# GNN layer on one core: gamma in a wider centring matmul, and the loaded-column matmuls of the last three panels behind the row-tiled ones

## The chip, the cores and the metric

The kernel runs on one core of one Trainium2 chip. The metric is the device time of one execution in microseconds (us); the kernel before takes 407.3 us, the median of three runs (407.11 to 409.26).

## What is computed

All numbers are float32. N is 5120 nodes (2048 users, 3072 items), the embedding has 64 elements.

```python
h = jnp.maximum(_layernorm(x, axis=-1), 0.0)
# in the layer, with ego = res = h
u = par_u[0] * par_u[1] * (diag_u[:, None] * ego_u @ W_u) + ego_u
i = par_i[0] * par_i[1] * (diag_i[:, None] * ego_i @ W_i) + ego_i
e = jnp.concatenate([u, i], axis=0)
h = adj @ (adj.T @ e)
mu = jnp.mean(h, axis=-1, keepdims=True)
var = jnp.var(h, axis=-1, keepdims=True)
out = (h - mu) * jax.lax.rsqrt(var + LN_EPS) * ln_gamma + ln_beta + res
x = x + out
```

`adj` is 5120 x 5120, about 105 MB, and each element is used twice: in `t = adj.T @ e` and in `adj @ t`.

## The kernel before, in words

**Panels.** The columns of `adj` are cut into 20 panels of 256. For a panel, SP's queue loads five blocks of 1024 rows (`natural`, 1 MB each, L173), so that rows are on partitions, and for the last block the same numbers a second time with columns on partitions (`cols`, 1 MB, L177). Both have two buffers, picked by `a = g % 2`.

**A panel on TensorE.** `first` (L463) multiplies all five blocks with `e` and sums into `t_acc`: 40 matmuls of 256 columns, which write the two halves of the output partitions in turn. ScalarE copies the sum (`t_across`, L275), TensorE turns it (`t_turn`, L475), VectorE folds it into `t` (L379), and ScalarE spreads that over the four partition quadrants (`t_strips`, held in `centred`, L283). Then the panel is multiplied with `t` into `h_acc`: the first four row blocks by `second_strips` (L500), 64 matmuls in tiles of 32 rows, whose data VectorE has turned in 32 x 32 pieces (`strips`, L374); the fifth by `second_loaded` (L485), four matmuls of 512 columns straight from `cols`. In `step(g)` the order on TensorE is: `first(g)`, `second_loaded(g-1)`, `t_turn(g)`, `second_strips(g-1)`. Steps 2 to 17 are a loop with two panels in its body, 18 is written once more by `middle_steps` (L130 to L134), and panel 19, which is `LAST`, is written out at L555 to L565.

**The end.** `h_acc` now holds the transpose of h: banks 0 to 3 row blocks 0 to 3, cut by quadrants, and bank 4 (`LOADED`) block 4. ScalarE and VectorE copy the four banks into `h_across` (L319, L419), which lies over a dead part of `natural`, in two halves. `out_turn(m)` (L528) multiplies each piece of 128 columns of block m with `centre`. That turns the data back and subtracts the mean in one matmul, since `centre` is the identity minus 1/64 inside each half; its result lies in one bank, given by `out_bank(m)`. Block 4 comes by way of `across` (L323). Then, for each of the five blocks m: ScalarE squares (L313), VectorE sums the squares (L342), ScalarE takes the root (L249), VectorE multiplies the centred rows with gamma (L425), takes the reciprocal of the root (L347) and multiplies with it (L429). GpSimd adds the result to the residual `xs` (L231; for block 4 VectorE does, L432), and SP sends 256 KB to HBM (L198). TensorE's order in this stretch: `second_loaded(18)`, `out_turn(0)`, `out_turn(1)`, `second_loaded(19)`, `out_turn(2)` to `out_turn(4)`.

**What sets the order.** Each engine's program is written out by hand; engines meet only at semaphores. SP issues the loads in order: `load_natural(g, m)` waits for `first(g-2, m)` and for VectorE's turning of that block; `load_cols(g)` waits until `second_loaded` has been done g - 1 times. A late wait there holds back all loads behind it. The matmuls of float32 appear in the trace as two records each, with a weight load before each record.

Of the kernel before, what the change touches and what calls it, by code (L numbers as in the profile page):

```python
# [5 lines left out]
P = 128  # L6
N = 5120
D = 64
N_USERS = 2048
Q = 32  # L10
QUADRANTS = P // Q
ROWS = 1024
GROUPS = N // ROWS
# [23 lines left out]
def gnn_layer(nc, x, small, adj_rows, adj_cols, out):  # L37

    ctx = ExitStack()
    with ctx:  # L40
# [15 lines left out]
        ident = sb("ident", [P, P])  # L56
        centre = sb("centre", [P, P])
        smalls = sb("smalls", [P, SMALL])
# [18 lines left out]
        t_across = sb("t_across", [P, WIDE])  # L77
        t = sb("t", [P, 2, BLOCKS, D])
        t_strips = centred

        h_acc = ps("h_acc", [P, GROUPS, BANK])
# [5 lines left out]
        s_natural = [[sem(f"s_natural{a}{m}") for m in range(GROUPS)] for a in range(2)]  # L87
        s_cols = [sem(f"s_cols{a}") for a in range(2)]
        s_eps = sem("s_eps")
        s_idle = sem("s_idle")  # L90
# [32 lines left out]
        s_o_centred = sem("s_o_centred")  # L123
        s_o_gamma = sem("s_o_gamma")
        s_o_scaled = sem("s_o_scaled")
# [19 lines left out]

        def out_bank(m):

            return (t_acc[:, 0], t_acc[:, 1], h_acc[:, 0], h_acc[:, 1], h_acc[:, 2])[m]

# [17 lines left out]
        @block.sync  # L167
        def _(sp):
            sp.dma_start(xs[:, 0:GT, :], x[:, 0:GT, :]).then_inc(s_x[0], 16)
            sp.dma_start(smalls[:], small).then_inc(s_small, 16)  # L170

            def load_natural(g, m):
                sp.dma_start(natural[:, g % 2, m].rearrange("p t c -> p (t c)"),  # L173
                             adj_rows[g, m]).then_inc(s_natural[g % 2][m], 16)

            def load_cols(g):
                sp.dma_start(cols[:, g % 2].rearrange("p s b c -> p (s b c)"),  # L177
                             adj_cols[g]).then_inc(s_cols[g % 2], 16)

            for m in range(GROUPS):  # L180
                for g in range(2):
                    load_natural(g, m)
            for g in range(2):
                load_cols(g)
            for g in range(2, PANELS):
                for m in range(GROUPS):
                    sp.wait_ge(s_first, firsts_0(g - 2, m) if g < 4 else firsts(g - 2, m))
                    if m < TURNED:
                        sp.wait_ge(s_strips, TURNED * (g - 2) + m + 1)
                    load_natural(g, m)  # L190
                sp.wait_ge(s_loaded_done, g - 1)
                load_cols(g)
            for m in range(GROUPS):
                if m < LOADED:
                    sp.wait_ge(s_o_added, m + 1)
                else:
                    sp.wait_ge(s_o_done, 1)
                sp.dma_start(out[:, rows_of(m), :], xs[:, rows_of(m), :]).then_inc(s_out, 16)  # L198
            sp.wait_ge(s_out, 16 * GROUPS)

        @block.gpsimd
        def _(pool):
# [5 lines left out]
                                    pattern=[[-1, P]], channel_multiplier=1).then_inc(s_ident, 1)  # L208
            nc.gpsimd.memset(centre[:], 0.0).then_inc(s_zero, 1)
            for m in range(GROUPS):  # L210
# [12 lines left out]
            for d in range(2):  # L223
                half = slice(D * d, D * (d + 1))
                nc.gpsimd.memset(centre[half, half], -1.0 / D).then_inc(s_centre_part, 1)
            pool.wait_ge(s_centre_part, 2)
            nc.gpsimd.affine_select(out=centre[:], in_=centre[:], compare_op=ALU.not_equal, fill=1.0 - 1.0 / D,
                                    base=0, pattern=[[-1, P]], channel_multiplier=1).then_inc(s_centre, 1)
            for m in range(LOADED):
                pool.wait_ge(s_o_scaled, m + 1)  # L230
                nc.gpsimd.tensor_tensor(residual(m), scaled[:, m % 2].rearrange("p (k s) d -> p k s d", s=2),  # L231
                                        residual(m), ALU.add).then_inc(s_o_added, 1)

        @block.scalar
        def _(act):
# [41 lines left out]
            def spread_t(g, a):  # L277

                act.wait_ge(s_t, g + 1)
                for c in range(QUADRANTS):  # L280
                    for q in range(QUADRANTS):
                        into = t_strips[Q * q:Q * (q + 1), a].rearrange("p (b c) d -> p b c d", c=QUADRANTS)
                        last = nc.scalar.copy(into[:, :, c], t[Q * c:Q * (c + 1), a])  # L283
                last.then_inc(s_t_strips, 1)
# [21 lines left out]
            middle_steps(act, step)  # L306
            step(LAST, LAST % 2, LAST // 2)

            def square_out(m):
                n = GROUPS + m  # L310
                act.wait_ge(s_o_centred, m + 1)
                act.wait_ge(s_var, n - 1)
                nc.scalar.activation(squares[:, n % 2], out_bank(m).rearrange("p (k d) -> p k d", d=D),  # L313
                                     ACT.Square).then_inc(s_squares, 1)
                std(n)

            act.wait_ge(s_strips_last, 1)
            for half in range(2):
                nc.scalar.copy(*strips_across(half, 0)).then_inc(s_o_low, 1)  # L319
            square_out(0)  # L320
            square_out(1)
            act.wait_ge(s_loaded_done, PANELS)
            nc.scalar.copy(across[:, 0], h_acc[:, LOADED]).then_inc(s_o_loaded, 1)  # L323
            for m in range(2, GROUPS):
                square_out(m)

        @block.vector
        def _(dve):
# [47 lines left out]

            def keep_t(g, a):
                dve.wait_ge(s_t_turned, g + 1)
                nc.vector.tensor_reduce(t[:, a], t_turned[:, 0:2 * WIDE // 2].rearrange("p (b s d) -> p b d s",  # L379
                                                                                       b=BLOCKS, s=2),  # L380
                                        AX.X, ALU.add).then_inc(s_t, 1)

            def step(g, a, half):
                for m in range(TURNED):
                    turn_strips(g, a, half, m)
                keep_t(g, a)

# [23 lines left out]
            for g in range(2):  # L411
                keep_t(g, g)
            for m in range(TURNED):
# [4 lines left out]
            for half in range(2):  # L418
                nc.vector.tensor_copy(*strips_across(half, 2)).then_inc(s_o_high, 1)  # L419
            gamma_rows = gamma_s.unsqueeze(1).to_broadcast([P, GT, D])  # L420
            for m in range(GROUPS):
                sum_squares(GROUPS + m)
                if m >= 2:
                    dve.wait_ge(s_o_added, m - 1)
                nc.vector.tensor_tensor(scaled[:, m % 2], out_bank(m).rearrange("p (k d) -> p k d", d=D),  # L425
                                        gamma_rows, ALU.mult).then_inc(s_o_gamma, 1)
                r = inverse_deviation(GROUPS + m)
                dve.wait_ge(s_o_gamma, m + 1)
                nc.vector.tensor_tensor(scaled[:, m % 2], scaled[:, m % 2], r, ALU.mult).then_inc(s_o_scaled, 1)  # L429
            dve.wait_ge(s_o_scaled, GROUPS)  # L430
# [5 lines left out]
        def _(pe):  # L436
# [42 lines left out]
            def second_loaded(g, a, half):  # L479

                pe.wait_ge(s_cols[a], 16 * (half + 1))
                pe.wait_ge(s_t, g + 1)
                for b in range(BLOCKS):
                    for s in range(2):
                        last = nc.tensor.matmul(h_acc[D * s:D * (s + 1), LOADED], t[:, a, b, :], cols[:, a, s, b],  # L485
                                                start=(isinstance(g, int) and g == 0 and b == 0),
# [20 lines left out]
            def step(g, a, half):  # L507
                for m in range(GROUPS):
                    first(g, a, half, m)
                second_loaded(g - 1, 1 - a, half - 1 + a)  # L510
                t_turn(g)
                second_strips(g - 1, 1 - a).then_inc(s_strips_done, 1)

            def out_turn(m):

                if m == 0:
                    pe.wait_ge(s_centre, 1)
                    pe.wait_ge(s_t_across, PANELS)
                if m == LOADED:
                    pe.wait_ge(s_o_loaded, 1)  # L520
                else:
                    half = 0 if m < 2 else 1
                    pe.wait_ge(s_o_low, half + 1)
                    pe.wait_ge(s_o_high, half + 1)
                for k in range(HALF):
                    part = across[:, 0, P * k:P * (k + 1)] if m == LOADED else h_across[:, m, k].rearrange(
                        "p q i -> p (q i)")
                    last = nc.tensor.matmul(out_bank(m)[:, P * k:P * (k + 1)], part, centre[:], start=True, stop=True)  # L528
                last.then_inc(s_o_centred, 1)
# [25 lines left out]
            for m in range(GROUPS):  # L555
                first(LAST, LAST % 2, LAST // 2, m)
            t_turn(LAST)
            second_strips(LAST - 1, 0).then_inc(s_strips_done, 1)
            second_strips(LAST, 1).then_inc(s_strips_last, 1)
            second_loaded(LAST - 1, 0, LAST // 2)  # L560
            out_turn(0)
            out_turn(1)
            second_loaded(LAST, 1, LAST // 2)
            for m in range(2, GROUPS):
                out_turn(m)  # L565

# [35 lines left out]
```

## Time and profile before

| | |
|---|---|
| median of 3 runs | 407.3 us |
| profiled execution | 407.53 us |
| its span, first to last instruction | 405.7 us |
| mean granted TensorE clock | 0.986 |
| TensorE matmul busy | 382.7 us (94%) |
| VectorE busy | 219.6 us (54%) |
| ScalarE busy | 125.6 us (31%) |
| GpSimd busy | 19.9 us (5%) |
| HBM read | 127.36 MB |

The busy share is an average over the span; the stretch that the change touches begins at about 356 us, where it has to be read anew. PE is TensorE's matmuls, PEld its weight loads, DVE VectorE, ACT ScalarE, POOL GpSimd, SP the engine that issues the loads. The ends of matmul records are modelled.

### The profile page before, as it was taken

The page shows a single profiled execution, that of the slowest core. Times are in us where ns is not written, and L with a number is a line of the kernel's source. Part 1 is how long each engine was busy: PE and PEld are TensorE (multiplying, and loading weights), DVE is VectorE, ACT ScalarE, POOL GpSimd, SP SyncE. Part 2 cuts the span into 40 slices and gives each one's busy share as a digit, 9 for nine tenths or more (in the row PEclk, how much of TensorE's full clock was granted, in tenths as well). Part 3 has the DMA queues.
Part 4 walks back from the last instruction along what each step waited for, and adds up shares of the span by engine and source line. Part 5 has one row for each costly group of instructions (what it writes and reads, how often), then busy time and mean ns, then how long its engine had stood idle before and what let it go on. Part 6 is the DMA issues. An engine that isn't in the chain of part 4 may idle for free.

```text
span 405.7 us, 10226 instructions
## 1 busy us (share of the span) xinstructions
PE 382.7 (94%) x4524; PEld 197.0 (49%) x4524; DVE 219.6 (54%) x160; ACT 125.6 (31%) x410; POOL 19.9 (5%) x26
## 2 busy tenths in 40 slices
PE   5679799999999999999999999999999999999991
PEld 2446345455454645445464545546354554535451
DVE  5677658365471827446281735538183653719047
ACT  4434550413405041331504042250504224050422
POOL 1211700000000000000000000000000000000013
PEclk9989989999999999999999999999999999999997
DMA  8999895979897987979797897979789797940003
GB/s 315 422 422 419 331 417 211 357 299 395 329 428 292 387 332 304 414 295 427 291 420 300 327 392 300 428 284 428 296 348 376 291 427 291 426 155 2 3 1 129
DMA packets 18879, 128.89 MB, mean 318 GB/s; under 512 B 2096, under 2 KB 2224, under 8 KB 3504
## 3 DMA queue, kind: packets, MB, share of 16 engines
q1 hardware_dynamic: 18288, 127.63, 77.7%
q10 hardware_dynamic: 576, 1.05, 0.7%
q8 instruction: 11, 0.18, 0.2%
q14 instruction: 4, 0.03, 0.0%
HBM read 127.36 MB, written 1.31 MB: 317 GB/s over the span
## 4 chain that ended last, share of the span: by engine, by line
PE 87%; DVE 6%; ACT 4%; issue 2%; DMA 1%; DVEq 0%; ACTq 0%
PE t_acc L463 41%; PE h_acc L500 35%; PE h_acc L485 8%; ACT h_in L260 2%; PE t_turned L475 2%; ACT centred L283 1%; DVE var L342 1%; DMA xs<-x 1%; DVE scaled L429 1%; DVE e L366 1%; DVE scaled L425 1%; DVE strips L374 1%; DVE total L331 0%; PE h_acc L443 0%; DVE centred L337 0%
## 5 line engine op out<-in xcount | busy, mean ns | idle before, releaser
L374 DVE STREAM_TRANSPOSE strips<-natural 128x2048 f32<-128x2048 f32 x80 | 178.1, 2281 | 118.8 <-PE h_acc L500 118.8
L463 PE MATMUL t_acc<-natural,e 128*64 128x256 f32 x1600 | 180.6, 383 | 6.0 <-DVE e L366 6.0
L463 PEld LDWEIGHTS t_acc<-natural,e 128*64 128x64 f32 x1600 | 112.4, 137 | 77.8 <-issue 16.0
L500 PE MATMUL h_acc<-strips,centred 32*64 32x512 f32 x2560 | 143.9, 596 | 2.7 <-ACT centred L283 2.7
L283 ACT COPY centred<-t 32x128 f32<-32x128 f32 x320 | 94.5, 295 | 41.3 <-DVE t L379 37.7
L500 PEld LDWEIGHTS h_acc<-strips,centred 32*64 32x64 f32 x2560 | 55.9, 133 | 77.8 <-issue 77.8
L275 ACT COPY t_across<-t_acc 128x256 f32<-128x256 f32 x20 | 7.4, 372 | 195.8 <-PE t_acc L463 194.0
L485 PE MATMUL h_acc<-cols,t 128*64 128x512 f32 x160 | 37.9, 594 | 0.0
L379 DVE TENSOR_REDUCE t<-t_turned 128x128 f32<-128x256 f32 x20 | 8.5, 425 | 35.0 <-PE t_turned L475 35.0
L231 POOL TENSOR_TENSOR xs<-scaled,xs 128x512 f32<-128x512 f32 x4 | 5.1, 1272 | 347.2 <-DVE scaled L429 347.2
L485 PEld LDWEIGHTS h_acc<-cols,t 128*64 128x64 f32 x160 | 11.2, 137 | 15.0 <-issue 12.4
L475 PEld LDWEIGHTS t_turned<-ident,t_across 128*128 128x128 f32 x40 | 4.0, 140 | 15.9 <-issue 14.2
L260 ACT ACTIVATE h_in<-centred,rstd 128x64 f32<-128x64 f32 x40 | 10.2, 337 | 0.0
L337 DVE SCALAR_TENSOR_TENSOR centred<-total,xs 128x512 f32<-128x512 f32 x5 | 6.7, 1348 | 6.1 <-ACT h_in L260 6.1
L475 PE MATMUL t_turned<-ident,t_across 128*128 128x128 f32 x40 | 8.7, 300 | 1.1 <-DVE t L379 0.6
L419 DVE COPY natural<-h_acc 128x512 f32<-128x512 f32 x2 | 1.3, 686 | 13.6 <-PE h_acc L500 13.6
L213 POOL TENSOR_TENSOR xs<-xs,h_in 128x512 f32<-128x512 f32 x5 | 6.3, 1267 | 33.6 <-ACT h_in L260 33.6
L342 DVE TENSOR_REDUCE var<-squares 128x8 f32<-128x512 f32 x10 | 6.7, 674 | 2.2 <-ACT squares L313 2.2
L536 PE MATMUL h_acc<-across 32*64 32x512 f32 x64 | 5.2, 803 | 1.8 <-POOL across L204 1.8
L269 ACT COPY across<-h_acc 128x512 f32<-128x512 f32 x5 | 2.9, 581 | 12.3 <-PE h_acc L443 12.3
L453 PE MATMUL h_acc<-smalls,across 128*128 128x128 f32 x40 | 5.8, 287 | 0.9 <-ACT across L269 0.9
L218 POOL TENSOR_TENSOR xs<-xs,smalls 128x512 f32<-128x512 f32 x5 | 6.2, 1267 | 0.0
(39 smaller groups left out, 58.7 us busy)
## 6 DMA issues: line engine op xcount, KB each, us to landing
natural<-adj_rows SPq DMA_DIRECT2D x100, 1024.0 KB, 10.9
cols<-adj_cols SPq DMA_DIRECT2D x20, 1024.0 KB, 4.8
out<-xs SPq DMA_DIRECT2D x5, 256.0 KB, 2.0
xs<-x ACTq DMA_DIRECT2D x4, 256.0 KB, 5.9
xs<-x SPq DMA_DIRECT2D x1, 256.0 KB, 3.5
smalls<-small SPq DMA_DIRECT2D x1, 214.0 KB, 4.2
```

The source lines that it names most:

```text
L213: nc.gpsimd.tensor_tensor(xs[:, rows_of(m), :], xs[:, rows_of(m), :], h_in[:, m % 2], ALU.add).then_inc(s_res_part, 1)
L260: last = nc.scalar.activation(h_in[:, m % 2, k], centred[:, m % 2, k], ACT.Relu, scale=rstd[:, m % 2, k:k + 1])
L275: nc.scalar.copy(t_across[:], t_acc[:, a, 0:WIDE]).then_inc(s_t_across, 1)
L283: last = nc.scalar.copy(into[:, :, c], t[Q * c:Q * (c + 1), a])
L337: nc.vector.scalar_tensor_tensor(centred[:, m % 2], by_tile(total[:, m % 2]), -1.0 / D, xs[:, rows_of(m), :], ALU.mult, ALU.add).then_inc( ...
L342: nc.vector.tensor_reduce(var[:, n % 2], squares[:, n % 2], AX.X, ALU.add).then_inc(s_var, 1)
L374: nc.vector.transpose(strips[:, a, :, m].rearrange("p c t i -> p t c i"), natural[:, a, m].rearrange("p t (c j) -> p t c j", j=Q)).then_in ...
L379: nc.vector.tensor_reduce(t[:, a], t_turned[:, 0:2 * WIDE // 2].rearrange("p (b s d) -> p b d s", b=BLOCKS, s=2), AX.X, ALU.add).then_inc( ...
L463: last = nc.tensor.matmul(t_acc[D * s:D * (s + 1), a, 0:WIDE], e[:, GT * m + HALF * s + k, :], natural[:, a, m, HALF * s + k], start=(m == ...
L475: last = nc.tensor.transpose(t_turned[:, P * b:P * (b + 1)], t_across[:, P * b:P * (b + 1)], ident[:])
L485: last = nc.tensor.matmul(h_acc[D * s:D * (s + 1), LOADED], t[:, a, b, :], cols[:, a, s, b], start=(isinstance(g, int) and g == 0 and b == 0),
L500: last = nc.tensor.matmul(h_acc[D * s:D * (s + 1), q], t_strips[part, a, c, :], rows, start=(isinstance(g, int) and g == 0 and c == 0), st ...
```

## The change

- **Gamma.** `centre` becomes twice as wide. Its first 128 columns are as before, its second 128 columns are the same matrix with each column multiplied by its gamma (made once on GpSimd, behind the building of `centre`). `out_turn` multiplies with all 256 columns, so it gives the centred rows and, beside them, the centred rows times gamma. The result of a block now takes a pair of banks (`out_banks`). ScalarE squares the first part. VectorE multiplies the second part with the reciprocal; its own multiplication by gamma (L425) is gone.
- **Waits for banks.** `out_turn(1)` waits for both halves of the copies, `out_turn(3)` for the scaling of block 0, and `out_turn(4)` for that of block 1.
- **Order.** `step(18)` no longer calls `second_loaded(17)`. At the end TensorE runs `second_loaded(17)`, `out_turn(0)`, `out_turn(1)`, `second_loaded(18)`, `out_turn(2)`, `out_turn(3)`, `second_loaded(19)`, `out_turn(4)`. `t` gets a third buffer, used by panel 19.
- **The last load of columns.** The column-major data of panel 19 goes into `cols_last`, which lies over `natural[:, 0, 1]`, and is loaded when `first(18, 1)` and the turning of that block are done, not when `second_loaded` has been done 18 times.

The core of the diff (semaphore declarations, slices of `centre` and the passing of the buffer number left out):

```diff
-        def out_bank(m):
-
-            return (t_acc[:, 0], t_acc[:, 1], h_acc[:, 0], h_acc[:, 1], h_acc[:, 2])[m]
+        def out_banks(m):
+
+            pair = (t_acc[:, 0:2], h_acc[:, 0:2], h_acc[:, 2:4], t_acc[:, 0:2], h_acc[:, 0:2])[m]
+            return pair.rearrange("p n (k f c) -> p (n k) f c", k=2, f=2)
...
-                sp.wait_ge(s_loaded_done, g - 1)
-                load_cols(g)
+                if g < LAST:
+                    sp.wait_ge(s_loaded_done, g - 1)
+                    load_cols(g)
+            sp.wait_ge(s_first, firsts(LAST - 1, 1))
+            sp.wait_ge(s_strips, TURNED * (LAST - 1) + 2)
+            sp.dma_start(cols_last.rearrange("p s b c -> p (s b c)"), adj_cols[LAST]).then_inc(s_cols_last, 16)
...
+            pool.wait_ge(s_centre, 1)
+            nc.gpsimd.tensor_tensor(centre[:, 1].rearrange("p (s d) -> p s d", s=2),
+                                    centre[:, 0].rearrange("p (s d) -> p s d", s=2),
+                                    gamma_s.unsqueeze(1).to_broadcast([P, 2, D]), ALU.mult).then_inc(s_centre, 1)
...
-                nc.scalar.activation(squares[:, n % 2], out_bank(m).rearrange("p (k d) -> p k d", d=D),
+                nc.scalar.activation(squares[:, n % 2].rearrange("p (k s) d -> p k (s d)", s=2), out_banks(m)[:, :, 0],
...
-            square_out(0)
-            square_out(1)
-            act.wait_ge(s_loaded_done, PANELS)
-            nc.scalar.copy(across[:, 0], h_acc[:, LOADED]).then_inc(s_o_loaded, 1)
-            for m in range(2, GROUPS):
+            for m in range(GROUPS):
+                if m == LOADED:
+                    act.wait_ge(s_loaded_done, PANELS)
+                    nc.scalar.copy(across[:, 0], h_acc[:, LOADED]).then_inc(s_o_loaded, 1)
                 square_out(m)
...
-                nc.vector.tensor_tensor(scaled[:, m % 2], out_bank(m).rearrange("p (k d) -> p k d", d=D),
-                                        gamma_rows, ALU.mult).then_inc(s_o_gamma, 1)
-                r = inverse_deviation(GROUPS + m)
-                dve.wait_ge(s_o_gamma, m + 1)
-                nc.vector.tensor_tensor(scaled[:, m % 2], scaled[:, m % 2], r, ALU.mult).then_inc(s_o_scaled, 1)
+                nc.vector.tensor_tensor(scaled[:, m % 2].rearrange("p (k s) d -> p k s d", s=2),
+                                        out_banks(m)[:, :, 1].rearrange("p k (s d) -> p k s d", s=2), r,
+                                        ALU.mult).then_inc(s_o_scaled, 1)
...
-                second_loaded(g - 1, 1 - a, half - 1 + a)
+                if not isinstance(g, int):
+                    second_loaded(g - 1, 1 - a, half - 1 + a)
...
+                if m == 1:
+                    pe.wait_ge(s_o_low, 2)
+                    pe.wait_ge(s_o_high, 2)
+                if m >= 3:
+                    pe.wait_ge(s_o_scaled, m - 2)
...
-                    last = nc.tensor.matmul(out_bank(m)[:, P * k:P * (k + 1)], part, centre[:], start=True, stop=True)
+                    last = nc.tensor.matmul(out_banks(m)[:, k], part, centre[:], start=True, stop=True)
...
-            second_loaded(LAST - 1, 0, LAST // 2)
+            second_loaded(LAST - 2, 1, LAST // 2 - 1)
             out_turn(0)
             out_turn(1)
+            second_loaded(LAST - 1, 0, LAST // 2)
+            out_turn(2)
+            out_turn(3)
             second_loaded(LAST, 1, LAST // 2)
-            for m in range(2, GROUPS):
-                out_turn(m)
+            out_turn(LOADED)
```

## Rows read from the trace of the kernel before

**Rows 1.** The profile's page, part 2: tenths in 40 slices of the span.

```profile
PE   5679799999999999999999999999999999999991
DVE  5677658365471827446281735538183653719047
PEclk9989989999999999999999999999999999999997
```

**Rows 2.** Chain of waits, 355 to 375 us: start us, us, what.

```profile
355.92 1.72 PE h_acc L485 x8
357.64 0.37 PE t_turned L475 x2
358.01 7.05 PE h_acc L500 x128
365.06 8.81 PE t_acc L463 x80
373.87 0.02 issue
373.89 0.38 ACT t_across L275
374.27 0.04 issue
374.32 0.44 PE t_turned L475 x2
```

**Rows 3.** Chain of waits, the end.

```profile
392.30 0.69 DVE var L342
392.98 0.60 DVE scaled L425
393.58 0.12 DVE rstd L347
393.72 0.69 DVE scaled L429
394.42 0.60 DVE var L342
...
401.84 0.70 DVE scaled L429
402.54 0.02 issue
402.57 0.69 DVE xs L432
```

**Rows 4.** Instructions in order of time, the end: start us, us, engine, line.

```profile
388.60 1.94 PE L485 MATMUL h_acc<-cols,t 128*64 128x512 f32 x8
390.47 2.05 PE L528 MATMUL t_acc<-centre,natural 128*128 128x128 f32 x16
391.67 0.60 ACT L313 ACTIVATE squares<-t_acc 128x512 f32<-128x512 f32 x1 [1.81 <-PE t_acc L528]
392.45 1.94 PE L485 MATMUL h_acc<-cols,t 128*64 128x512 f32 x8
392.90 0.68 DVE L425 TENSOR_TENSOR scaled<-t_acc,smalls 128x512 f32<-128x512 f32 x1
393.02 0.30 ACT L249 ACTIVATE var<-var,eps 128x8 f32<-128x8 f32 x1 [0.75 <-DVE var L342]
393.50 0.19 DVE L347 RECIPROCAL rstd<-var 128x8 f32<-128x8 f32 x1
395.26 0.56 ACT L323 COPY across<-h_acc 128x512 f32<-128x512 f32 x1
396.21 1.06 PE L528 MATMUL h_acc<-centre,across 128*128 128x128 f32 x8
```

**Rows 5.** Busy time by stretch: window, us, PE, PEld, DVE, ACT, POOL, clock, DMA share, GB/s.

```profile
388.60:397.40 8.80, 8.67 (x64) 5.58 (x56) 6.33 (x12) 4.05 (x10) 2.15 (x2) 1.00 0.08 31
397.40:405.70 8.30, 0.00 (x0) 0.00 (x0) 5.72 (x12) 1.54 (x4) 2.94 (x3) 0.71 0.33 126
```

**Rows 6.** Instructions in order of time, 364.5 to 374.5 us.

```profile
364.99 8.85 PE L463 MATMUL t_acc<-natural,e 128*64 128x256 f32 x80
365.24 8.89 DVE L374 STREAM_TRANSPOSE strips<-natural 128x2048 f32<-128x2048 f32 x4 [6.77 <-PE h_acc L500]
```

**Rows 7.** Instructions in order of time: SP and DVE, 340 to 358 us.

```profile
340.19 2.65 SPq L173 DMA_DIRECT2D natural<-adj_rows  x5
347.32 6.70 DVE L374 STREAM_TRANSPOSE strips<-natural 128x2048 f32<-128x2048 f32 x3 [6.77 <-PE h_acc L500]
357.68 0.33 SPq L177 DMA_DIRECT2D cols<-adj_cols  x1
```

**Rows 8.** DMAs of L173 (340 to 343 us) and L177 (357 to 358 us).

```profile
DMA to landing us min/median/max: 6.9/10.9/14.6
DMA to landing us min/median/max: 4.7/4.7/4.7
```

**Rows 9.** Instructions of one line (L528, L485, L463): ns min/median/max, first and last start.

```profile
L528 PEld LDWEIGHTS t_acc<-centre,natural x16: 186/192/192, 390.5 to 392.1; 128*128 128x128 f32 x16
L528 PE MATMUL t_acc<-centre,natural x16: 275/275/377, 390.5 to 392.2; 128*128 128x128 f32 x16
L485 PE MATMUL h_acc<-cols,t x16: 592/592/643, 388.6 to 393.8; 128*64 128x512 f32 x16
L463 PE MATMUL t_acc<-natural,e x80: 379/379/430, 365.0 to 373.5; 128*64 128x256 f32 x80
```

**Rows 10.** GpSimd, start of the span: the work behind which the widening stands.

```profile
49.25 0.29 POOL L227 TENSOR_SCALAR_AFFINE_SELECT centre<-centre 128x128 f32<-128x128 f32 x1
```

More of the change, by code:

```diff
@@ L56, in gnn_layer @@
         ident = sb("ident", [P, P])
-        centre = sb("centre", [P, P])
+        centre = sb("centre", [P, 2, P])
         smalls = sb("smalls", [P, SMALL])
@@ L77, in gnn_layer @@
         t_across = sb("t_across", [P, WIDE])
-        t = sb("t", [P, 2, BLOCKS, D])
+        t = sb("t", [P, 3, BLOCKS, D])
         t_strips = centred
+        cols_last = natural[:, 0, 1].rearrange("p t c -> p (t c)").rearrange("p (s b c) -> p s b c", s=2, b=BLOCKS)
         h_acc = ps("h_acc", [P, GROUPS, BANK])
@@ L88, in gnn_layer @@
         s_cols = [sem(f"s_cols{a}") for a in range(2)]
+        s_cols_last = sem("s_cols_last")
         s_eps = sem("s_eps")
@@ L123, in gnn_layer @@
         s_o_centred = sem("s_o_centred")
-        s_o_gamma = sem("s_o_gamma")
         s_o_scaled = sem("s_o_scaled")
@@ L208, in _ @@
                                     pattern=[[-1, P]], channel_multiplier=1).then_inc(s_ident, 1)
-            nc.gpsimd.memset(centre[:], 0.0).then_inc(s_zero, 1)
+            nc.gpsimd.memset(centre[:, 0], 0.0).then_inc(s_zero, 1)
             for m in range(GROUPS):
@@ L224, in _ @@
                 half = slice(D * d, D * (d + 1))
-                nc.gpsimd.memset(centre[half, half], -1.0 / D).then_inc(s_centre_part, 1)
+                nc.gpsimd.memset(centre[half, 0, half], -1.0 / D).then_inc(s_centre_part, 1)
             pool.wait_ge(s_centre_part, 2)
-            nc.gpsimd.affine_select(out=centre[:], in_=centre[:], compare_op=ALU.not_equal, fill=1.0 - 1.0 / D,
+            nc.gpsimd.affine_select(out=centre[:, 0], in_=centre[:, 0], compare_op=ALU.not_equal, fill=1.0 - 1.0 / D,
                                     base=0, pattern=[[-1, P]], channel_multiplier=1).then_inc(s_centre, 1)
+            pool.wait_ge(s_centre, 1)
+            nc.gpsimd.tensor_tensor(centre[:, 1].rearrange("p (s d) -> p s d", s=2),
+                                    centre[:, 0].rearrange("p (s d) -> p s d", s=2),
+                                    gamma_s.unsqueeze(1).to_broadcast([P, 2, D]), ALU.mult).then_inc(s_centre, 1)
             for m in range(LOADED):
@@ L279, in spread_t @@
                 act.wait_ge(s_t, g + 1)
+                into_t = t[:, 2 if isinstance(g, int) and g == LAST else a]
                 for c in range(QUADRANTS):
@@ L282, in spread_t @@
                         into = t_strips[Q * q:Q * (q + 1), a].rearrange("p (b c) d -> p b c d", c=QUADRANTS)
-                        last = nc.scalar.copy(into[:, :, c], t[Q * c:Q * (c + 1), a])
+                        last = nc.scalar.copy(into[:, :, c], into_t[Q * c:Q * (c + 1)])
                 last.then_inc(s_t_strips, 1)
@@ L306, in _ @@
             middle_steps(act, step)
-            step(LAST, LAST % 2, LAST // 2)
+            step(LAST, 1, LAST // 2)
             def square_out(m):
@@ L375, in turn_strips, with keep_t @@
                                     natural[:, a, m].rearrange("p t (c j) -> p t c j", j=Q)).then_inc(s_strips, 1)
-            def keep_t(g, a):
+            def keep_t(g, a, into):
                 dve.wait_ge(s_t_turned, g + 1)
-                nc.vector.tensor_reduce(t[:, a], t_turned[:, 0:2 * WIDE // 2].rearrange("p (b s d) -> p b d s",
+                nc.vector.tensor_reduce(t[:, into], t_turned[:, 0:2 * WIDE // 2].rearrange("p (b s d) -> p b d s",
                                                                                        b=BLOCKS, s=2),
@@ L385, in step @@
                     turn_strips(g, a, half, m)
-                keep_t(g, a)
+                keep_t(g, a, 2 if isinstance(g, int) and g == LAST else a)
             row_sums(0)
@@ L411, in _ @@
             for g in range(2):
-                keep_t(g, g)
+                keep_t(g, g, g)
             for m in range(TURNED):
@@ L419, in _ @@
                 nc.vector.tensor_copy(*strips_across(half, 2)).then_inc(s_o_high, 1)
-            gamma_rows = gamma_s.unsqueeze(1).to_broadcast([P, GT, D])
             for m in range(GROUPS):
                 sum_squares(GROUPS + m)
+                r = inverse_deviation(GROUPS + m).rearrange("p (k s) d -> p k s d", s=2)
                 if m >= 2:
                     dve.wait_ge(s_o_added, m - 1)
-                nc.vector.tensor_tensor(scaled[:, m % 2], out_bank(m).rearrange("p (k d) -> p k d", d=D),
-                                        gamma_rows, ALU.mult).then_inc(s_o_gamma, 1)
-                r = inverse_deviation(GROUPS + m)
-                dve.wait_ge(s_o_gamma, m + 1)
-                nc.vector.tensor_tensor(scaled[:, m % 2], scaled[:, m % 2], r, ALU.mult).then_inc(s_o_scaled, 1)
+                nc.vector.tensor_tensor(scaled[:, m % 2].rearrange("p (k s) d -> p k s d", s=2),
+                                        out_banks(m)[:, :, 1].rearrange("p k (s d) -> p k s d", s=2), r,
+                                        ALU.mult).then_inc(s_o_scaled, 1)
             dve.wait_ge(s_o_scaled, GROUPS)
@@ L479, in second_loaded @@
             def second_loaded(g, a, half):
-                pe.wait_ge(s_cols[a], 16 * (half + 1))
+                if isinstance(g, int) and g == LAST:
+                    pe.wait_ge(s_cols_last, 16)
+                    lhs, rhs = t[:, 2], cols_last
+                else:
+                    pe.wait_ge(s_cols[a], 16 * (half + 1))
+                    lhs, rhs = t[:, a], cols[:, a]
                 pe.wait_ge(s_t, g + 1)
@@ L484, in second_loaded @@
                     for s in range(2):
-                        last = nc.tensor.matmul(h_acc[D * s:D * (s + 1), LOADED], t[:, a, b, :], cols[:, a, s, b],
+                        last = nc.tensor.matmul(h_acc[D * s:D * (s + 1), LOADED], lhs[:, b, :], rhs[:, s, b],
                                                 start=(isinstance(g, int) and g == 0 and b == 0),
@@ L516, in out_turn @@
                 if m == 0:
-                    pe.wait_ge(s_centre, 1)
+                    pe.wait_ge(s_centre, 2)
                     pe.wait_ge(s_t_across, PANELS)
@@ L555, in _ @@
             for m in range(GROUPS):
-                first(LAST, LAST % 2, LAST // 2, m)
+                first(LAST, 1, LAST // 2, m)
             t_turn(LAST)
```

## The prediction

> **What bounds the kernel now.** I read the slices of the page first: TensorE is at 9 tenths or more from the seventh slice to the last but one, at full clock, and in the last slice it is at 1 while VectorE is at 7 [rows 1]. So there are two stretches with different limits, and the change touches both. The chain of waits says where they meet. Up to 388.6 us it is TensorE matmul after matmul [rows 2]; from 392.3 us to the end it is VectorE, which does four operations for each of the five blocks of the output: the sum of squares, gamma, the reciprocal, the scaling [rows 3]. A block begins every 2.1 us there (392.30, 394.42; over all four steps it is 2.03). In between stand the matmuls of the end in order of time [rows 4]. TensorE's last record ends at 396.21 + 1.06 = 397.27, and VectorE's last at 402.57 + 0.69 = 403.26. The table by stretch shows the same: TensorE is busy for 8.67 of the 8.80 us up to 397.4 and not at all afterwards [rows 5]. So VectorE bounds the end, but TensorE is full until shortly before it. The question is what happens when VectorE's work is cut and TensorE's is raised there.
>
> **Part 1: `second_loaded(17)` leaves step 18.** It takes 1.72 us of the chain, and then `t_turn` follows with 0.37: 2.09 from 355.92 to 358.01 [rows 2]. But it also hid ScalarE's copy of `t_across`, for which `t_turn` waits. Panel 19 already runs without cover: 0.02 + 0.38 + 0.04 of waiting and then 0.44, together 0.88 [rows 2]. The step is shortened by 2.09 - 0.88 = **1.21 us**. Bounds: 0, if another wait takes its place, to 1.72, if the copy cost nothing. I take 1.21, since panel 19 is the same sequence without cover.
>
> What could be late 1.21 us earlier? The four turnings of panel 19 start when the strips of panel 17 are done (365.24, 0.2 behind them) and take 8.89 us beside the 8.81 us of `first(19)` [rows 2, 6]. Both ends move together. The `natural` blocks of panel 19 were issued from 340.19 on and landed after 14.6 us at most; even counted from the last issue (342.84) that is 357.4, and `first(19)` would need them at 365.06 - 1.21 = 363.85 [rows 2, 7, 8].
>
> **Part 2: the last load of columns.** It was issued at 357.68 and landed 4.7 us later [rows 7, 8]. Now it waits for the second turning of panel 18; three began at 347.32 and took 6.70, so the second ends near 351.8. That is earlier than before, while the `natural` blocks are still landing, and may push the last of them back by its own 4.7 us at most, to 362.1, still before 363.85. It is itself wanted at about 398 (part 4) and not at 392.45. Nothing behind it on SP's queue is wanted before the first output. Cost 0 to 0; had it no cover, up to 4.7.
>
> **Part 3: the centring matmuls.** This is the term that decides. A block has four matmuls, eight records. Sixteen records of 128 columns start from 390.47 to 390.47 + 2.05 - 0.275 = 392.25, which is 0.10 once and then 0.112 a record [rows 4, 9]. A 256-column record with the full array is not in the trace. The nearest rows are L463: 256 columns, 128 rows, but half of the output partitions, two records side by side. 80 records start within 8.85 - 0.38 = 8.47 us, so 40 pairs have 0.215 us each [rows 6, 9]. The `cols` matmuls have 512 columns, and eight records (four pairs) take from 388.60 to 390.47 with the change of form, 0.43 a pair [rows 4]. So a pass costs 0.84 ns a column in both, and 0.112 us is what 128 columns cost at that price, plus 0.005. The durations say the same of the full array: 275 ns for 128 columns, 379 for 256 and 592 for 512, which is 104 and 213 more for 128 and 256 more columns [rows 9]. The ends are modelled, but the engine that waits confirms the 275: the eighth centring record ends at 390.47 + 0.10 + 7 x 0.112 + 0.275 = 391.63, and ScalarE starts at 391.67 [rows 4]. Bounds for a wide record: 0.112 (the wider stream costs nothing, because something else sets the 0.112) and 0.215. I take 0.215. A block then takes 1.72 us of TensorE and not 0.89, five of them 4.1 us more.
>
> The page "TensorE: Matmul & The Clock Gate" of the Trainium skill speaks for the other bound. Its section on LDWEIGHTS gives the columns divided by 1.2 ns, 107 ns for 128 columns, as much as the spacing of the centring records; its section on the back-to-back gap gives N/2.4 + 2.5 ns, 109 ns for N = 256. By the two together the weight load would set the pace and the second 128 columns would be free. The trace disagrees with the gap as far as it goes: 256 columns stand at 215 ns and 512 at 430. No row of a full-array record decides it, so it stays a rival.
>
> **Part 4: the end put together**, on the old time axis, without part 1. `second_loaded(17)` stands where that of 18 stood, 388.60 to 390.47, and covers the copies as before. A pair of blocks in the wide form takes 0.10 + 16 x 0.215 + 0.10 for the change of form = 3.64, where the narrow pair took 392.45 - 390.47 = 1.98. So `second_loaded(18)` starts at 394.11, `out_turn(2)` at 395.98 (+1.87), `second_loaded(19)` at 399.62, and its last record ends at 401.56 (+1.94) [rows 4]. ScalarE's copy for block 4 (0.56 [rows 4]), with 0.04 on each side, lets `out_turn(4)` start at 402.20. Its last record starts 0.10 + 7 x 0.215 = 1.61 later and takes 0.38: 404.19. Then +0.04 the square, and +0.63 from there to the sum (391.67 to 392.30): 404.86. From the sum on nothing hides anything: 0.72 to the root (392.30 to 393.02), 0.30 root and 0.04, 0.19 reciprocal and 0.03 (before, only 0.12 of the reciprocal was outside cover), 0.72 scaling with its hand-over (401.84 to 402.57), 0.69 the residual: 2.69 [rows 3, 4]. End 407.55, where it was 403.26: **+4.29 us**.
>
> Is VectorE the bound instead? Without gamma its period is 0.72 + 0.30 + 0.04 + 0.22 + 0.69 less the 0.1 overlap of the next sum, 1.88: the root on ScalarE, which gamma had hidden, comes into the open, and of gamma's 0.68 only 0.15 a block is saved. Five blocks from 392.30 + 0.83 (the first block is also late by 0.83) bring the fifth sum to 400.65. TensorE's 404.86 is later by 4.2. The waits for `s_o_scaled` 1 and 2 are met near 395.1 and 397, before `out_turn(3)` (397.7) and `out_turn(4)`: 0.
>
> Two small things: ScalarE's copy stands behind the root of block 3. That block's matmuls end near 399.7, square and sum take it to 401.2, the root to 401.6, a tie with 401.56; up to 0.1. And GpSimd's widening of `centre` comes behind L227 at 49.25 [rows 10], 340 us before it is used, and is hidden: 0.
>
> **Sum.** -1.21 + 4.29 = +3.08 us, to which the 0.1 of the tie gives 3.1. Behind VectorE's last instruction the same 256 KB output follows. 407.53 + 3.1 = 410.6; the profiled execution lies 0.2 above the median of the runs, so 410.5 as a median.
>
> **Rivals.**
> 1. *The wide stream is free* (0.112 a record). `second_loaded(18)` starts at 392.45, that of 19 at 396.30 and ends at 398.24; `out_turn(4)` starts at 398.88 and ends at 400.04; sum at 400.71, end at 403.40. That is +0.14 - 1.21 = -1.07, and 406.3 as a median: not slower. For it: 0.112 is at one form only, and the weight loads between the records keep the same spacing (390.5 to 392.1 for sixteen), so it could be they that set it [rows 9]. Against it: the durations and L463. It is decided by the price of a record, since 39 of them stand on the path to the end of `out_turn(4)` behind the first: with 1.07 us in hand the break-even is 0.112 + 1.07/39 = 0.14, and 0.5% (2.0 us) slower is crossed at 0.19.
> 2. *The middle gives nothing*: another wait, such as the turning on VectorE (8.89 beside 8.81 [rows 2, 6]), takes the place of `second_loaded(17)`. Then 410.5 + 1.2 = 411.7. Against it: VectorE starts its turnings at the end of the strips, which moves too.
> 3. *The clock falls in the end.* It was 1.00 until 397.4, with TensorE 8.67 of 8.80 us busy, and fell only after TensorE had stopped [rows 5]. TensorE now works on to 404, with a hole of 0.6 before `out_turn(4)`. At the lower level (1.2 GHz) that block's 1.7 us would double: 412.2. The whole end shows no reason for it.
> 4. *The DMA*: the early column load displaces `natural` by more than its own time: up to 411.5; the two slacks above speak against it.
>
> **How the numbers follow.** Forecast 0.80, own range 409.7 to 411.4. Rival 1 0.12, with the prices in between, 406.3 to 409.5. Rivals 2 and 4 together 0.05, rival 3 0.03. The range 409.1 to 411.9 leaves out rival 1 nearly whole and the far end of rival 3. About 0.5% (2.0 us) is what a measurement of this kernel can tell from no change: slower from 409.3 on. Slower 0.77 (the forecast but for the part that noise in the runs could take under 409.3, and rivals 2 to 4), same 0.19 (rival 1 and that part), faster 0.04 (rival 1 with a middle that gives more).
>
> **What would show it.** Right: L528's records, now 128x256, at 379 ns and 0.215 apart; no L485 between L463 and L475 of panel 18, with 0.4 us of waiting for L275 there; the strips of panel 19 ending 1.2 us earlier, at 387.4; TensorE busy almost to 403; VectorE idle before each sum; the chain of the end going through L485 and L528 of block 4. Wrong: wide records 0.112 apart; L485 of panel 19 waiting for `cols_last`; VectorE's period still the chain of the end; the end of the last strips where it was.

## Result and profile after

The changed kernel takes 410.48 us (median of 20 executions, 408.61 to 412.46), the kernel before 407.25 us (20, 405.21 to 409.26). The ratio is 1.0076, 95% interval 1.0055 to 1.0098: slower by 3.1 us (2.2 to 4.0). That is over the 0.5% that the prediction named as what can be told from no change. The numbers in the table are read from one profiled execution of each kernel.

| profiled execution | before | after |
|---|---|---|
| span | 405.7 us | 409.4 us |
| first(18)'s end to the end of the last strips | 32.75 | 31.55 |
| from there to VectorE's last instruction | 14.59 | 18.95 |
| TensorE's last record, behind the last strips | 8.6 | 15.6 |
| VectorE busy, share of the span | 54% | 53% |

The second and third row are read from the chain of waits. First its part around panel 18 in the kernel after (start us, us, what), to be compared with [rows 2]:

```profile
356.48 0.02 issue
356.50 0.38 ACT t_across L285
356.88 0.04 issue
356.92 0.44 PE t_turned L483 x2
357.36 7.05 PE h_acc L513 x128
364.41 8.81 PE t_acc L471 x80
```

The 1.72 us of `second_loaded` are gone, and the wait for ScalarE's copy stands in their place, as panel 19 had it before. From 356.48 to 357.36 are 0.88 us, where [rows 2] had 2.09. Nothing behind it became later.

Then the end of the same chain, to be compared with [rows 3]:

```profile
374.11 13.92 PE h_acc L513 x256
388.03 1.87 PE h_acc L498 x8
389.89 1.93 PE t_acc L547 x8
391.82 1.73 PE h_acc L547 x8
393.55 1.87 PE h_acc L498 x8
395.41 1.92 PE h_acc L547 x8
397.34 1.73 PE t_acc L547 x8
399.06 1.89 PE h_acc L498 x8
...
400.98 0.59 ACT across L334
401.57 0.04 issue
401.62 2.01 PE h_acc L547 x8
...
403.65 0.61 ACT squares L324
...
404.28 0.70 DVE var L352
...
405.00 0.31 ACT var L259
...
405.33 0.21 DVE rstd L357
...
405.57 0.70 DVE scaled L435
...
406.29 0.69 DVE xs L440
```

VectorE's five blocks are no longer in the chain; only the last one is. In front of it stands TensorE with three blocks of columns (1.87 to 1.89) and five centrings: 1.73 behind another centring, 1.92 or 1.93 behind a block of columns, 2.01 for the last, which follows a wait of 0.67 for ScalarE's copy. All this, the wait included, goes from 388.03 to 403.62, which is 15.6 us. The pieces follow each other without a gap but for that one wait, so the new waits for banks cost TensorE nothing that the chain shows. The centring records by line (ns min/median/max, first and last start), to be compared with [rows 9]:

```profile
L547 PEld LDWEIGHTS t_acc<-centre,natural x16: 186/190/190, 389.8 to 398.5; 128*128 128x128 f32 x16
L547 PE MATMUL t_acc<-centre,natural x16: 379/379/483, 389.8 to 398.7; 128*128 128x256 f32 x16
```

They take 379 ns, as long as the 256-column records of half the output partitions in [rows 9], and not 275. The ends of these records are modelled, but their starts say the same: eight records take 1.73 us in the chain, 0.216 each.

What VectorE waits for now, in order of time (start us, us, engine, line; the bracket is the idle time before it):

```profile
392.49 0.69 DVE L352 TENSOR_REDUCE var<-squares 128x8 f32<-128x512 f32 x1 [3.06 <-ACT squares L324]
...
393.54 0.20 DVE L357 RECIPROCAL rstd<-var 128x8 f32<-128x8 f32 x1 [0.37 <-ACT var L259]
...
398.00 0.69 DVE L352 TENSOR_REDUCE var<-squares 128x8 f32<-128x512 f32 x1 [1.65 <-ACT squares L324]
...
404.28 0.69 DVE L352 TENSOR_REDUCE var<-squares 128x8 f32<-128x512 f32 x1 [2.40 <-ACT squares L324]
```

It waits 0.37 us for the root of its own block, which gamma used to hide, and 1.65 and 2.40 us ahead of the sums of blocks 2 and 4, whose squares wait for TensorE. The last load of columns was issued at 352.42, landed 7.5 us later, is first read at 398.99, and is not in the chain:

```profile
352.42 0.33 SPq L198 DMA_DIRECT2D natural<-adj_cols  x1
```

**The rest of the span.** The span grew by 3.7 us, the two stretches by -1.20 + 4.36 = 3.16. The rest is from the start: `first(18)` ends at 356.48 and not at 355.92, 0.56 later. The change does not touch that part but for one small instruction on GpSimd. By stretch (window, us, PE, PEld, DVE, ACT, POOL, clock, DMA share, GB/s), the first 60 us of the kernel before:

```profile
0.00:60.00 60.00, 45.93 (x424) 24.38 (x424) 39.88 (x47) 28.28 (x91) 14.85 (x22) 0.94 0.96 387
```

and of the kernel after:

```profile
0.00:60.00 60.00, 47.68 (x416) 25.54 (x424) 39.87 (x47) 28.29 (x91) 15.31 (x23) 0.91 0.92 370
```

VectorE and ScalarE do the same in both, while TensorE's granted clock is 0.94 in one and 0.91 in the other, and it is busy for 1.75 us more. I take the 0.56 for chance of the execution: in the profiles of the kernels below, six of which have that GpSimd instruction and none another change in the start, the start came out both shorter and longer than in the kernel before (last section). So the effect of the change is 3.16 us, and the ratio (3.1) and the difference of the medians (3.2) agree with it.

### The profile page after: what moved, and what is told of

It is laid out like the page before. It is cut to its first block, busy times and chain, and to the rows that moved or that the text cites. A ratio compares the mean times of both kernels' runs of the same rounds, so it can differ in the third digit from the quotient of the medians.

```text
span 409.4 us, 10223 instructions
## 1 busy us (share of the span) xinstructions
PE 389.7 (95%) x4524; PEld 200.9 (49%) x4524; DVE 217.2 (53%) x155; ACT 126.2 (31%) x410; POOL 20.4 (5%) x27
## 4 chain that ended last, share of the span: by engine, by line
PE 89%; ACT 4%; DVE 2%; issue 2%; DMA 1%; DVEq 0%; ACTq 0%
PE t_acc L471 42%; PE h_acc L513 34%; PE h_acc L498 8%; ACT h_in L270 2%; PE t_turned L483 2%; PE h_acc L547 1%; ACT centred L294 1%; PE t_acc L547 1%; DMA xs<-x 1%; DVE e L376 1%; PE h_acc L451 1%; DVE centred L347 0%; DVE var L352 0%; DVE total L341 0%; ACT t_across L285 0%
## 5 line engine op out<-in xcount | busy, mean ns | idle before, releaser
L513 PE MATMUL h_acc<-strips,centred 32*64 32x512 f32 x2560 | 142.2, 590 | 2.7 <-ACT centred L294 2.7
L498 PE MATMUL h_acc<-cols,t 128*64 128x512 f32 x152 | 36.0, 594 | 0.0
L555 PE MATMUL h_acc<-across 32*64 32x512 f32 x64 | 6.5, 976 | 1.8 <-POOL across L210 1.8
L461 PEld LDWEIGHTS h_acc<-smalls,across 128*128 128x128 f32 x40 | 5.4, 211 | 2.6 <-ACT across L279 1.5
```

Of the source, the lines that this page charges most:

```text
L461: last = nc.tensor.matmul(h_acc[:, m, P * b:P * (b + 1)], across[:, m % 2, P * b:P * (b + 1)], wdiag[:, int(m >= USER_GROUPS)], start=True ...
L498: last = nc.tensor.matmul(h_acc[D * s:D * (s + 1), LOADED], lhs[:, b, :], rhs[:, s, b], start=(isinstance(g, int) and g == 0 and b == 0), ...
L513: last = nc.tensor.matmul(h_acc[D * s:D * (s + 1), q], t_strips[part, a, c, :], rows, start=(isinstance(g, int) and g == 0 and c == 0), st ...
```

## Experiments

For each, the two stretches of the table above are given ("middle" and "end", for the kernel before 32.75 and 14.59), since they are free of the start. They come from one profile a kernel. Where two kernels should agree in a stretch they do so to 0.01 us (31.55 or 31.56 in five kernels, 32.75 in three), so I read differences of 0.1 us from them. The measured ratios to the kernel before stand beside them; their intervals are 0.4% to 0.5% wide, which is 1.6 to 2.2 us. The diffs are cuts, against the changed kernel, but for two whose text says against what.

### Only the wide centring

The order of matmuls, loads and ScalarE's copy as before; the gamma part is as changed. Of the edit only TensorE's order is shown.

```diff
-            second_loaded(LAST - 2, 1, LAST // 2 - 1)
+            second_loaded(LAST - 1, 0, LAST // 2)
             out_turn(0)
             out_turn(1)
-            second_loaded(LAST - 1, 0, LAST // 2)
-            out_turn(2)
-            out_turn(3)
             second_loaded(LAST, 1, LAST // 2)
-            out_turn(LOADED)
+            for m in range(2, GROUPS):
+                out_turn(m)
```

> Only the wide centring, in the old order of matmuls and loads. Theory A (the 256-column records cost 0.216 us where the 128-column ones cost 0.112, and TensorE, not VectorE, then ends last): from the end of the last strips, out_turn(2) to out_turn(4) run from 395.98 on the old axis without a break, the last ends at 401.43, and VectorE ends at 404.8 where it was 403.26: +1.5 us against the kernel before, with the step of panel 18 unchanged. Rival B (the order is what costs, the width little): within 0.5 us of before. Neither gives more than half of the +3.2 of the whole change.

Middle 32.75, end 16.46: +1.87 us. Ratio 1.0019 (0.9994 to 1.0043); the stretches say 1.0046, just above the interval, whose executions also hold the changing start. This is the one kernel where the two disagree by more than the interval, and that stays open. TensorE ran as forecast, but the end was 0.33 longer than expected (VectorE's end at 404.8 where it was 403.26, +1.54), and against the expectation it was VectorE that bounded the last two blocks:

```profile
398.95 0.70 DVE var L348
...
399.67 0.31 ACT var L255
...
400.00 0.21 DVE rstd L353
...
400.24 0.69 DVE scaled L431
400.93 0.60 DVE var L348
...
401.55 0.31 ACT var L255
...
401.89 0.21 DVE rstd L353
...
402.12 0.69 DVE scaled L431
402.82 0.60 DVE var L348
```

From block 2 on VectorE is again the bound: its sums start 1.89 apart (400.93, 402.82), TensorE's blocks come every 1.73. That is the period that the prediction gave to VectorE without gamma, 1.88, and it beats 2.03 by only 0.15. So the width alone makes TensorE deliver later, and VectorE catches up nearly nothing of it.

### Only the order

Centring 128 columns wide and gamma on VectorE as before, without the new waits for banks; all else as changed. Of the edit the matmul is shown.

```diff
-                    last = nc.tensor.matmul(out_banks(m)[:, k], part, centre[:], start=True, stop=True)
+                    last = nc.tensor.matmul(out_bank(m)[:, P * k:P * (k + 1)], part, centre[:, 0], start=True, stop=True)
```

> Only the order (second_loaded(17) to the end, the late load of columns, ScalarE's copy for block 4 behind block 3), with the centring 128 columns wide and gamma on VectorE. Theory A: -1.21 us in the step of panel 18. In the end ScalarE copies block 4 only behind the root of block 3 (399.40 on the old axis), out_turn(4) runs 400.04 to 401.20, and the fifth sum starts at 401.87 where it was 400.42: +1.45. Together +0.2 us against before. Rival B (the order is what costs): +2 us or more.

Middle 31.55, end 15.92: -1.20 + 1.33 = +0.13 us. Ratio 0.9997 (0.9975 to 1.0019). The middle is as in the changed kernel. What was gained there is given back at the end, and the chain names the place:

```profile
397.17 0.61 DVE var L352
...
397.80 0.03 ACT var L259
397.82 0.18 issue
398.01 0.57 ACT across L334
398.58 0.04 issue
398.63 1.17 PE h_acc L544 x8
```

ScalarE's copy for block 4 waits on its engine behind the root of block 3, which waits for VectorE's sum of block 3; TensorE stands still for the copy.

### The order, and ScalarE's copy earlier

As the kernel with only the order, but ScalarE copies block 4 between the square and the root of block 3.

```diff
-                if m == LOADED:
+                if m == LOADED - 1:
+                    act.wait_ge(s_o_centred, m + 1)
+                    act.wait_ge(s_var, GROUPS + m - 1)
+                    nc.scalar.activation(squares[:, (GROUPS + m) % 2], ...)
                     act.wait_ge(s_loaded_done, PANELS)
                     nc.scalar.copy(across[:, 0], h_acc[:, LOADED]).then_inc(s_o_loaded, 1)
-                square_out(m)
+                    std(GROUPS + m)
+                else:
+                    square_out(m)
```

> As the order alone, but ScalarE copies block 4 between the square and the root of block 3. Theory A: the copy then starts when second_loaded(19) is done (398.28 on the old axis), the fifth sum at 400.71: +0.29 and -1.21, together -0.9 us against before. If instead TensorE's fourth block of columns itself were the limit of the end, the copy's place would change nothing and it would be as the order alone (+0.2).

Middle 31.55, end 14.92: -0.87 us. Ratio 0.9972 (0.9947 to 0.9996). One place in ScalarE's order was worth 1.00 us, and the extra block of columns at the end costs 0.33 and not 1.87, since TensorE had the rest in hand.

### The changed kernel with the narrow centring, gamma left out

This one leaves gamma out of the result, and the waits for banks too; it shows what the changed kernel would be if the second 128 columns were free.

```diff
-                                        out_banks(m)[:, :, 1].rearrange("p k (s d) -> p k s d", s=2), r,
+                                        out_bank(m).rearrange("p (k s d) -> p k s d", s=2, d=D), r,
```

> The changed kernel with the centring 128 columns wide again and gamma left out of the result altogether: what the wide stream costs, all else as changed. Theory A: VectorE's period is 1.9 us (the root is in the open), ScalarE's copy comes behind the root of block 3 at 399.0 on the old axis, and the end is at 404.1: +0.9 and -1.21, together -0.35 us against before and 3.5 below the changed kernel. Rival B (width costs little): at most 1 us below the changed kernel.

Middle 31.56, end 15.43: -0.35 us, as expected. Ratio 0.9993 (0.9973 to 1.0012). The width alone, all else as changed, thus costs 18.95 - 15.43 = 3.52 us, against 3.5 expected. Its chain again has the copy behind the root of block 3:

```profile
399.04 0.03 ACT var L258
399.06 0.18 issue
399.25 0.57 ACT across L333
399.82 0.04 issue
399.86 1.17 PE h_acc L541 x8
```

### The kernel before with the cover split

The diff is against the kernel before. Besides what it shows, ScalarE copies block 4 between the square and the root of block 3, as in the kernel with the early copy.

```diff
-            second_loaded(LAST - 1, 0, LAST // 2)
+            second_loaded(LAST - 1, 0, LAST // 2, range(0, 1))
             out_turn(0)
             out_turn(1)
+            second_loaded(LAST - 1, 0, LAST // 2, range(1, 2))
+            out_turn(2)
+            out_turn(3)
             second_loaded(LAST, 1, LAST // 2)
-            for m in range(2, GROUPS):
-                out_turn(m)
+            out_turn(LOADED)
```

> The kernel before, with narrow centring and gamma on VectorE; in the end only half of second_loaded(18) stands ahead of the first two centrings and half behind, blocks 2 and 3 are centred ahead of second_loaded(19), and ScalarE copies block 4 ahead of the root of block 3. Theory A (VectorE bounds the end of the kernel before and TensorE has over 2 us in hand there): VectorE's chain starts 0.86 us earlier, since the copies need 0.9 of the 1.87 us that the matmuls covered; the end is 0.86 shorter, 13.7 us from the last strips to VectorE's last and not 14.6. If TensorE bounded the end, splitting its work would give nothing.

Middle 32.75, end 13.72: -0.87 us. Ratio 0.9983 (0.9959 to 1.0007). In its chain the cover is 1.01 and not 1.87, and VectorE starts its first sum 2.76 behind the last strips instead of 3.63:

```profile
388.54 1.01 PE h_acc L490 x4
389.55 1.10 PE t_acc L534 x8
...
390.67 0.60 ACT squares L313
...
391.30 0.69 DVE var L347
```

VectorE is in the chain without a break from there on, so the other two moves in this edit (blocks 2 and 3 ahead of `second_loaded(19)`, the copy later) cost and gain nothing. Here VectorE is the bound, and what starts it earlier is worth its full size.

### The order with the cover split

`second_loaded(17)` is cut in the same way in the kernel with the order and the early copy, against which the diff is.

```diff
-            second_loaded(LAST - 2, 1, LAST // 2 - 1)
+            second_loaded(LAST - 2, 1, LAST // 2 - 1, range(0, 1))
             out_turn(0)
             out_turn(1)
+            second_loaded(LAST - 2, 1, LAST // 2 - 1, range(1, 2))
             second_loaded(LAST - 1, 0, LAST // 2)
```

> The order alone with the early copy, and second_loaded(17) split around the first two centrings. Theory A: there TensorE bounds the end (it works for 11.4 us behind the last strips), so starting VectorE 0.86 earlier gives nothing: the end stays at 14.9 us, within 0.15, and the whole at -0.9 against before. If VectorE still bounded the end, it would be 14.1.

Middle 31.55, end 14.92, the same as without the split. Ratio 0.9986 (0.9963 to 1.0009). The same edit that gave 0.87 gives 0.00 where TensorE is the bound.

### Half of the block moved

Half of `second_loaded(17)` stays in step 18, the other half is the cover at the end; narrow centring, gamma on VectorE, early copy.

```diff
-                if not isinstance(g, int):
-                    second_loaded(g - 1, 1 - a, half - 1 + a)
+                second_loaded(g - 1, 1 - a, half - 1 + a, range(1 if isinstance(g, int) else BLOCKS))
...
-            second_loaded(LAST - 2, 1, LAST // 2 - 1)
+            second_loaded(LAST - 2, 1, LAST // 2 - 1, range(1, 2))
```

> The order of the changed kernel with narrow centring and gamma on VectorE, but only half of second_loaded(17) goes to the end, as the cover of the copies; the other half stays in step 18 and covers ScalarE's copy of t_across. Theory A: -0.86 us in the middle; in the end VectorE starts 0.86 earlier, but the fifth block is late by 0.27 from TensorE: -0.59. Together -1.45 us against before and 1 us or less against the order alone with the early copy. If the middle gives nothing with the cover kept, -0.6.

Middle 31.89, end 14.06: -0.86 - 0.53 = -1.39 us. Ratio 0.9968 (0.9941 to 0.9994), median 405.86 us. This is the fastest of the versions: a third of a per cent faster than the kernel before. The kernel with the early copy (0.9972) also lies below 1 with its whole interval; by the stretches this one is 0.52 us faster still, which the ratios cannot tell apart. The middle of its chain:

```profile
356.38 0.86 PE h_acc L506 x4
357.24 0.37 PE t_turned L491 x2
```

Half a block (0.86) hides ScalarE's copy (0.38, with its two hand-overs 0.44) entirely. So moving the first half out gains its full 0.86; moving the second out as well gains only 0.34 more (31.55) and costs the end 0.86 (14.92).

## Why the prediction was right

The sum was right in each of its terms, and not only in its total. That the median (410.48) came within 0.02 us of the forecast (410.5) is luck, since executions spread over 4 us; that the two stretches gave 3.16 us where the sum had 3.1 is not.

- **Part 1** (-1.21): measured -1.20. The same sequence in panel 19 was the right row to read it from. Rival 2, a new wait in the middle, is refuted by every kernel with the new order: all have 31.55 or 31.56. The end of the last strips, which the prediction expected at 387.4, lies at 388.03 only because the start of this execution is 0.56 longer.
- **Part 2** (0): right; the load was issued 5 us earlier than the old one and waited for nowhere. It took 7.5 us to land and not 4.7, but had landed at 359.9, and `first(19)` started only at 364.41.
- **Part 3** (0.215 a wide record): the first two centrings take 3.66 in the chain (389.89 to 393.55), where the sum had 3.64. This is the term that carried the forecast. Its working was less exact than its value: 8.47 us over 40 pairs is 0.212, and not 0.215. In the trace of the kernel before, the first pair of `first(19)` is followed after 0.266 us and each later one after 0.216.
- **Part 4** (+4.29, and 0.1 for the tie): measured +4.36. The tie on ScalarE turned out as a tie: the root of block 3 ends at 400.92, the matmuls at 400.95, and the copy starts at 400.98, so of the 0.1 set aside for it nothing was needed. That VectorE would drop out of the chain but for the last block is what the trace shows. One sign was inexact: VectorE stands idle ahead of the sums of blocks 0, 2 and 4, and not ahead of each.
- **VectorE's new period** (1.88): seen as 1.89 in the kernel with only the wide centring.
- **Rival 1** (free stream) was refuted by the spacing of L547's records (0.216 us), by their 379 ns and by the narrow kernel without gamma. Its own number was wrong, though: -1.07 was forecast, -0.35 measured. I had let ScalarE copy block 4 at once and forgot that in the new order the copy stands behind the root of block 3, which ties TensorE to VectorE. In the forecast itself TensorE was late enough to hide it.
- **Rival 3** (the clock): no; by stretch the end of the kernel after has the clock at 1.00:

```profile
388.03:403.61 15.58, 14.89 (x64) 8.73 (x64) 7.42 (x14) 5.25 (x11) 5.08 (x4) 1.00 0.14 51
```

- **Rival 4** (the DMA): no trace of it; `first(19)` takes 8.81 us as before.

The two halves of the change are not additive: the order alone +0.13, the width alone +1.87, both +3.16. One reason is the time that TensorE had in hand. In the kernel before its last record ended at 397.27, so with 0.67 for the square and the hand-overs block 4's sum could have begun at 397.94; it began at 400.50 in the chain, 2.6 us later. Each half of the change was paid in part out of that. Together they put TensorE's last record 7.0 us later (8.6 to 15.6), which is 4.4 more than it had in hand, and the end grew by 4.36. The other reason is ScalarE's copy behind the root of block 3: it costs 1.00 us in the kernel with only the order, and nothing where TensorE is late.

## What to carry to other kernels

Work moved from the engine that bounds a stretch to its neighbour is paid at the neighbour's price: here about 0.15 us a block was gained on VectorE (2.03 to 1.89), since the removed operation had hidden another wait, for 0.83 us a block on TensorE. Before adding to an engine that is not in the chain, measure how long it stands still before the chain ends, and spend no more than that. And when work serves as cover for a copy, give it only the length of the copy: here half a block of matmuls covered as well as a whole one, in both places.

## What the runs showed of the hardware

The price per column of a float32 record was the same where one record fills the array and where two share it: 256 columns took 379 ns in both, and 0.216 us lay between the starts of two full-array records (L547) as between those of two pairs (L463). The section on the back-to-back gap of the Trainium skill's page "TensorE: Matmul & The Clock Gate" names no data type and gives N/2.4 + 2.5 ns for an isolated matmul, which is 0.109 us for 256 columns. The float32 records here stand twice as far apart, and the measurement decides.

Most executions of one kernel fall into groups 1.7 to 1.9 us apart. Of the 20 of the kernel before, five lie at 405.2 to 405.7, ten at 407.0 to 408.1, five at 408.9 to 409.3; of the kernel after five lie at 408.6 to 408.9, twelve at 410.1 to 411.2 and three at 412.3 to 412.5. In all nine profiles the time from the end of the first panel's strips to the end of `first(18)` is 295.54 to 295.58 us, while that end itself lies between 355.6 and 357.4. So the difference is made in the first 62 us.

The fastest group also has the highest granted clock: 0.993 over the span in all five executions of the kernel after, against 0.984 to 0.990 in the other fifteen. In one place the profiles show the price: the first panel's strips take 8.82 us in the chain of three kernels (before, only the order, narrow without gamma), where the granted clock from 50 to 60 us is 0.83, and 7.13 in the six others, where it is 1.00. The size of 1.69 us fits the groups, but these three are not the slowest three (the start is longest in one of them and short in the other two), so that the clock makes the groups is not shown. For effects of 1 us the stretches of the trace were the better measure.
